# Cross-attention with four head groups per round: row and column tiles of the array, the division on GpSimd, the maxima of the context moved

## What is computed

```python
h, d = 16, 8                                   # heads, channels of a head
q = layernorm_per_head(x @ Wq.T + bq) * d ** -0.5
k = layernorm_per_head(y @ Wk.T + bk);  v = y @ Wv.T + bv     # y: context, 512 keys
attn = einsum('bihd,bjhd->bhij', q, k)
attn = where(mask, attn, -inf)
out = einsum('bhij,bjhd->bihd', softmax(attn), v) @ Wo.T + bo
```

## Time and profile before

| what | value |
|---|---|
| median of 3 runs | 739.34 us (737.47 to 740.51) |
| the profiled execution | 740.16 us |
| its span, first to last instruction | 738.3 us |
| busy: PE, DVE, ACT, POOL | 618.2, 498.4, 306.1, 144.8 us |
| mean granted clock of TensorE | 0.763 |

### The profile page before, as it was taken

The page is one execution under the profiler, slowest core; times in us unless marked ns, Lnnn a source line. Parts: engine busy times, 40 slices in busy tenths (PEclk is TensorE's granted clock), DMA queues, the critical chain, the costliest instruction groups (busy, mean ns, idle before and its releaser), DMA issues.

```text
span 738.3 us, 21781 instructions
## 1 busy us (share of the span) xinstructions
PE 618.2 (84%) x8501; PEld 476.5 (65%) x8501; DVE 498.4 (68%) x1962; ACT 306.1 (41%) x859; POOL 144.8 (20%) x177
## 2 busy tenths in 40 slices
PE   4969997876889758999899998997689888988866
PEld 3536665434678558888888888886466556655634
DVE  1697665477453467777777777774287888878883
ACT  2935453433365543333333333333445445544511
POOL 3330000420800000000000000000543564346500
PEclk9999999887799855555555555555599999999997
DMA  9700000000100200000000000000000000000000
GB/s 344 321 1 1 1 1 2 1 1 2 41 1 1 66 22 3 0 0 0 0 0 0 0 0 0 0 0 1 0 1 1 0 1 1 1 0 1 0 1 7
DMA packets 6057, 15.26 MB, mean 21 GB/s; under 512 B 2640, under 2 KB 3288, under 8 KB 5504
## 3 DMA queue, kind: packets, MB, share of 16 engines
q1 hardware_dynamic: 5296, 11.19, 4.1%
q10 hardware_dynamic: 720, 3.55, 1.2%
HBM read 14.60 MB, written 0.13 MB: 20 GB/s over the span
## 4 chain that ended last, share of the span: by engine, by line
PE 49%; DVE 30%; ACT 11%; issue 8%; DMA 1%; POOL 1%; DVEq 0%; SPq 0%; ACTq 0%
PE bank L1659 9%; PE bank L1732 7%; PE bank L1568 6%; PE bank L1386 4%; PE bank L1369 4%; ACT esp L661 3%; PE bank L1519 2%; DVE ssum L1122 2%; DVE T L1192 2%; ACT a L647 2%; ACT e L663 2%; PE bank L1377 2%; PE bank L1506 2%; DVE rz L1159 2%; DVE zs L1157 2%
## 5 line engine op out<-in xcount | busy, mean ns | idle before, releaser
L1568 PE MATMUL bank<-esp,qblk 128*128 128x1 f16 (+1 forms) x2048 | 66.6, 166 | 0.7 <-ACT esp L661 0.7
L1568 PE MATMUL bank<-hsp,kT 128*128 128x2 f16 x2048 | 63.6, 166 | 2.5 <-DVE hsp L1150 1.7
L1568 PEld LDWEIGHTS bank<-hsp,kT 128*128 128x128 f16 x2048 | 60.0, 104 | 3.5 <-DVE hsp L1147 1.7
L1568 PEld LDWEIGHTS bank<-esp,qblk 128*128 128x128 f16 x2048 | 61.3, 104 | 1.3 <-ACT esp L661 1.1
L647 ACT ACTIVATE a<-opre 128x4 f32<-128x4 f32 x64 | 13.1, 205 | 115.8 <-DVE opre L1110 115.8
L455 POOL MEMSET ctxT<- 128x128 f32 x1 | 0.3, 312 | 306.2 <-DVE xres L1166 306.2
L1192 DVE SCALAR_TENSOR_TENSOR T<-bank,bct,T 128x256 f32<-128x256 f32 x112 | 46.4, 475 | 1.3 <-PE bank L1745 1.3
L1179 DVE TENSOR_TENSOR_SCAN qblk<-ctxT,bank 128x512 f32<-128x512 f32 x32 | 37.6, 1208 | 13.5 <-PE bank L1732 13.1
L1568 PE MATMUL bank<-asp,lsp 128*128 128x4 f16 x768 | 30.7, 168 | 16.4 <-DVE asp L1112 16.4
L1568 PEld LDWEIGHTS bank<-asp,lsp 128*128 128x128 f16 x768 | 25.4, 105 | 27.9 <-DVE asp L1112 27.7
L1179 DVE TENSOR_TENSOR_SCAN w<-kT,bank 128x512 f32<-128x512 f32 x32 | 37.5, 1207 | 8.2 <-PE bank L1732 8.2
(11 more groups left out here) (327 smaller groups left out, 1471.1 us busy)
## 6 DMA issues: line engine op xcount, KB each, us to landing
w<-in_w_dram SPq DMA_DIRECT2D x2, 2048.0 KB
ctxT<-in_ctxT_dram SPq DMA_DIRECT2D x8, 256.0 KB, 12.9
wqkv<-in_qkvT_dram ACTq DMA_DIRECT2D x1, 1536.0 KB, 11.7
w<-in_mw_dram SPq DMA_DIRECT2D x1, 1024.0 KB, 5.1
lw<-in_lw_dram SPq DMA_DIRECT2D x1, 960.0 KB, 19.8
rows<-in_rows_dram ACTq DMA_DIRECT2D x1, 772.0 KB, 7.9
wqkv<-in_fw_dram SPq DMA_DIRECT2D x1, 532.0 KB, 3.3
T<-in_mask_dram ACTq DMA_DIRECT2D x1, 512.0 KB, 5.8
```

The source lines that it names most:

```text
L1568: return pe.matmul(out, lhsT, rhs, start=start, stop=stop, skip_group_check=True)
```

## The change

All 16 heads of a sequence are now handled in one round of four items, which fill the array by tiles.

- Queries: `qblk` keeps one 128 x 128 block per sequence. Rows 32g to 32g+31 hold group g. Four multiplications fill it (with the negated scale) instead of sixteen, and GpSimd's zeroing (line 381) is gone.
- Scores: four matmuls of 32 rows each, on rows 32g to 32g+31 of the array, into banks 0 to 3, issued one behind the other. They wait for all four maxima of the sequence before, since there is one set of banks.
- Scores are negated, so that the mask operation's minimum is the negated maximum, and line 841 is gone; ACT's exponential has scale -1 and works in place.
- The multiplication by the reciprocal moves from DVE to GpSimd, in place; DVE keeps the reciprocal. Items have six buffers (XR).
- Of the four copies of transposed blocks ACT makes three and DVE the fourth, behind the round's maxima. Eight buffers.
- Values: one `x_pv` per sequence, two rounds late, whose 16 matmuls go over the four column tiles in turn.
- `wmean` is computed on DVE between the first and the second round; GpSimd's lines 405 and 411 come behind its 32 multiplications.
- The eight maxima of the context move into self-attention's loop, one per block m behind `a_rope`; those of the LSTM's weights and the gathering follow that loop, and `partition_all_reduce` comes behind GpSimd's eight additions.
- In the last layer two semaphores (`r_gate`, `r_h`) are merged into `f_gate` and `f_h`; nothing else changes there.

```diff
@@ gpsimd
-            pool.memset(qblk[:, :, :, :, :], 0.0).then_inc(sem["mask_ready"], 1)
...
+            for i in range(B * XG):
+                pool.wait_ge(sem["x_rz"], i + 1)
+                pool.tensor_scalar(x_soft(i), x_soft(i), xrz[:, i:i + 1], 0.0, ALU.mult, ALU.add).then_inc(sem["x_norm"], 1)
             pool.wait_ge(sem["a_wmean"], 1)
@@ scalar
-                if i >= 2:
-                    act.wait_ge(sem["x_norm"], i - 1)
-                act.activation(T[:, 2 + i % 2, :], T[:, i % 2, :], ACT.Exp, bias=xneg[:, i:i + 1],
+                act.activation(x_soft(i), x_soft(i), ACT.Exp, scale=-1.0, bias=xneg[:, i:i + 1],
                                accum_out=xz[:, i:i + 1]).then_inc(sem["x_exp"], 1)
...
-            for i in range(B * XG + 2):
+                if i >= 2 * XG:
+                    act.wait_ge(sem["x_pv"], i // XG - 1)
+                act.activation(x_probT(i), bank[4 + i % 2][:, :], ACT.Copy).then_inc(sem["x_pt"], 1)
+
+            for i in range((B + 1) * XG):
                 if i < B * XG:
                     x_exp(i)
-                if i >= 2:
-                    x_copy_pt(i - 2)
+                if i >= XG and i % XG != XG - 1:
+                    x_copy_pt(i - XG)
@@ vector
+                dve.tensor_scalar(qblk[:, 0, :, h, :], T[:, 10, 0:TOK].rearrange("p (b s) -> p b s", b=B),
+                                  cst[:, C_HM + h:C_HM + h + 1], -XD ** -0.5, ALU.mult, ALU.mult) \
...
+                if i >= XR:
+                    dve.wait_ge(sem["x_tr"], i - XR + 1)
+                dve.tensor_tensor_reduce(x_soft(i), bank[g][:, :], maskb[:, b * SK:(b + 1) * SK],
+                                         1.0, -FLOOR, ALU.add, ALU.min, xneg[:, i:i + 1]).then_inc(sem["x_max"], 1)
...
+                dve.reciprocal(xrz[:, i:i + 1], xz[:, i:i + 1]).then_inc(sem["x_rz"], 1)
...
+            for b in range(B + 2):
+                for g in range(XG):
+                    i = b * XG + g
+                    if i < B * XG:
+                        x_max(i)
+                    if 1 <= i <= B * XG:
+                        x_norm(i - 1)
+                if b == 0:
+                    dve.wait_ge(sem["d_attn"], 32)
+                    step(dve.tensor_reduce(wmean[:, :], wqkv[:, 0:2 * AH * AD].rearrange("p (h d) -> p h d", d=AD), AX, ALU.add))
+                    dve.tensor_scalar(wmean[:, :], wmean[:, :], 1.0 / AD, None, ALU.mult).then_inc(sem["a_wmean"], 1)
+                if 1 <= b <= B:
+                    x_copy_pt(b * XG - 1)
+                if b >= 2:
+                    x_heads(b - 2)
@@ vector, self-attention's loop
+                if m < B:
+                    l_size(lmax[:, m:m + 1], ctxT[:, m * SK:(m + 1) * SK])
@@ tensor
+                for g in range(XG):
+                    own = slice(32 * g, 32 * g + 32)
+                    pe.matmul(bank[g][:, :], qblk[own, 0, b, :, :], kT[own, b * SK:(b + 1) * SK],
+                              start=True, stop=True).then_inc(sem["x_score"], 1)
...
                 for c in range(KC):
+                    for g in range(XG):
+                        ins = pe.matmul(bank[6 + b % 2][32 * g:32 * g + 32, 0:P], vx[:, b * KC + c, 32 * g:32 * g + 32],
+                                        x_probT(b * XG + g)[:, c * P:(c + 1) * P], start=(c == 0), stop=(c == KC - 1))
...
+            for b in range(B + 2):
+                if b < B:
+                    x_scores(b)
+                if b >= 2:
+                    x_pv(b - 2)
+                if 1 <= b <= B:
+                    for g in range(XG):
+                        x_transpose((b - 1) * XG + g)
```

More of the change, by code:

```diff
@@ L331, in transposed, with x_soft, x_probT, x_turned @@
             return n + 1 if n < LN_LAST else LN_LAST + 1
+        def x_soft(i):
+            return T[:, i % XR, :]
+        def x_probT(i):
+            return T[:, XR + i % (2 * XG), :]
+        def x_turned(eng, i):
+            if i % XG == XG - 1:
+                eng.wait_ge(sem["x_ptd"], i // XG + 1)
+            else:
+                eng.wait_ge(sem["x_pt"], i // XG * (XG - 1) + i % XG + 1)
         def nth(stream, t):
@@ L427, in _ @@
                                    ALU.mult, ALU.add).then_inc(sem["a_z"], 1)
+            pool.wait_ge(sem["l_stat"], 1)
+            pool.partition_all_reduce(lall[:, :], ltop[:, :], P, REDUCE.max).then_inc(sem["l_max"], 1)
             pool.wait_ge(sem["x_res"], 2)
@@ L823, in _ @@
                 k_hat(s)
-                if s >= 1:
-                    q_blocks(2 * (s - 1))
-            dve.wait_ge(sem["d_attn"], 32)
-            step(dve.tensor_reduce(wmean[:, :], wqkv[:, 0:2 * AH * AD].rearrange("p (h d) -> p h d", d=AD), AX, ALU.add))
-            dve.tensor_scalar(wmean[:, :], wmean[:, :], 1.0 / AD, None, ALU.mult).then_inc(sem["a_wmean"], 1)
+                if 1 <= s <= 4:
+                    q_block(s - 1)
             def x_max(i):
-                b = i // XG
+                b, g = divmod(i, XG)
@@ L866, in l_size @@
                 step.mark(dve.tensor_reduce(to, of, AX, ALU.max, apply_absolute_value=True))
-            for i in range(B * XG + 4):
-                if i < B * XG:
-                    x_max(i)
-                if 1 <= i <= B * XG:
-                    x_norm(i - 1)
-                if i >= 4 and (i - 4) % XG == XG - 1:
-                    x_heads((i - 4) // XG)
-                if i < B:
-                    l_size(lmax[:, i:i + 1], ctxT[:, i * SK:(i + 1) * SK])
-                if i == 12:
-                    dve.wait_ge(sem["l_w"], 4)
-                    for k, (at, end) in enumerate(((14, 15), (13, 14), (4, 13))):
-                        l_size(lmax[:, B + k:B + k + 1], lw[:, at * D:end * D])
-            step.sync()
-            step(dve.tensor_reduce(ltop[:, 0:1], lmax[:, 0:B], AX, ALU.max))
-            dve.tensor_copy(ltop[:, 1:4], lmax[:, B:B + 3]).then_inc(sem["l_stat"], 1)
+            for b in range(B + 2):
[13 more added lines that the diff above has]
+                    x_heads(b - 2)
             dve.wait_ge(sem["x_oT"], B)
@@ L929, in _ @@
                     a_rope(m - 1)
+                if m < B:
+                    l_size(lmax[:, m:m + 1], ctxT[:, m * SK:(m + 1) * SK])
+            dve.wait_ge(sem["l_w"], 4)
+            for k, (at, end) in enumerate(((14, 15), (13, 14), (4, 13))):
+                l_size(lmax[:, B + k:B + k + 1], lw[:, at * D:end * D])
+            step.sync()
+            step(dve.tensor_reduce(ltop[:, 0:1], lmax[:, 0:B], AX, ALU.max))
+            dve.tensor_copy(ltop[:, 1:4], lmax[:, B:B + 3]).then_inc(sem["l_stat"], 1)
             dve.wait_ge(sem["a_rope"], 8)
```

90 lines of the change are left out of this document (32 added, 58 removed).

## The result

| what | before | after |
|---|---|---|
| median of all runs beside each other | 738.40 us (737.39 to 740.51, 4 runs) | 708.01 us (705.90 to 710.02, 4 runs) |
| ratio of the times, 95% interval | | 0.9585 [0.9548, 0.9621] |
| the profiled execution, its span | 740.16, 738.3 us | 708.04, 706.2 us |
| busy: PE, DVE, ACT, POOL | 618.2, 498.4, 306.1, 144.8 us | 574.1, 478.9, 299.5, 161.7 us |
| mean granted clock of TensorE | 0.763 | 0.748 |

What follows compares the result with a forecast made beforehand. PE alone was taken to bound cross-attention; after the change, a DVE-ACT loop of waits. Stage -30.2, bias +0.4 and maxima +2.3 sum to -27.5 us on 740.16, giving 712.7, forecast 713; range 706 to 727.

Steps and rivals of the forecast that it cites:

- the stage: Cross-attention, up to the last `x_heads`: predicted to end at 95.0 instead of 125.2 us, so -30.2 us.
- Scores and values: PE's tiled matmuls per sequence: scores 1.08 us instead of 4.24, values 0.97 instead of 3.96.
- The round: One sequence of four items in cross-attention: a loop of waits between DVE and ACT, 5.65 us.
- rival 3: Cross-attention rounds: shorter waits, a round takes ACT's 4.6 us, five rounds save 5, total 708; chance 0.08.
- They wait for nobody: Next sequence's scores on PE: start at the fourth maximum, long before needed, take 1.1 us, and wait for nobody.
- The third round at half clock: Cross-attention's third round: PE at half clock is the bound, 7.7 us with gaps, fourth maximum at 59.2.
- Rival 1: Cross-attention: clock stays at half, all rounds from the second on at 7.73 us, total 726; chance 0.18.
- Drain: End of cross-attention, from the last maximum through the last sequences' copies and heads: 7.6 us, to 95.0.
- The bias beside GpSimd: DVE's bias operation (line 886) behind cross-attention, slowed beside GpSimd's subtraction: +0.4 us, bounds 0 and 1.1.
- `partition_all_reduce` isn't needed until the third layer: 0: GpSimd's reduction over partitions, moved behind its eight additions: claimed to cost 0 us.
- The maxima in the loop: Context maxima on DVE in self-attention's loop: one of two fits idle time, +2.3 us over eight, bounds 0 and 5.6.
- The division on GpSimd at nothing: Cross-attention's division moved to GpSimd: 3.6 to 4.2 us per round beside 5.65, cost nothing unless above 1.4 each.

Runs made afterwards that it cites:

- memset late: Changed kernel with GpSimd's zeroing of qblk for self-attention moved behind its eight additions; 702.38 us, ratio 0.9513.
- division on VectorE: Changed kernel with the 32 divisions moved back from GpSimd to VectorE, in place behind each reciprocal; 715.6 us.
- heads later: Changed kernel with VectorE's two reductions that collect a sequence's heads moved behind the next round's first maximum and its reciprocal; 709.03 us, ratio 0.9584.
- maxima moved in the kernel before: Kernel before with only the maxima of context and weights, and GpSimd's reduction over partitions, moved in and behind self-attention's loop; 740.49 us, ratio 1.0015.
- two items later: Changed kernel with reciprocal and division two items behind the maximum instead of one; 707.62 us, ratio 0.9566.
- three banks: Changed kernel with three PSUM banks in turn for the transposes instead of two, and one for the values instead of two; 712.23 us, ratio 0.9629.
- both: Changed kernel with three PSUM banks for transposes, one for values, and reciprocal and division two items behind the maximum; 698.88 us, ratio 0.9465.

## Why the prediction was right, and where its steps were off

Forecast 713, measured 708.0, in the range. The sum said -27.5 us; the profiled executions differ by -32.1. The 4.6 us between them are misses of both signs: the stage gave 3.7 more, self-attention's loop cost 1.5 less, the rest gave 1.4, and the layer norm cost 2.0 more.

- **Scores and values: right.** 1.14 and 1.08 us for 1.08 and 0.97. The row nearest in form, which overlaps five times, pointed the right way; against 3.60 on the whole array the scores overlap 3.2 times. The pair of tiles would have given 1.97 for the values.
- **The round: 5.27, not 5.65.** The loop over VectorE and ScalarE was named rightly, but its terms were durations laid end to end. Their starts lie closer: the copy starts 0.72 us behind the exponential, the next exponential 0.49 behind the copy of 0.59, and the operation behind VectorE's copy of 0.69 starts 0.61 after it. Five rounds make 1.9 us. That is the small form of rival 3, whose bound of 4.6 wasn't reached.
- **"They wait for nobody": wrong.** Scores do wait, in TensorE's list behind transposes that wait for a bank, and VectorE's copy waits for these transposes too. It cost nothing in the sum, because that loop is as long as the other, which was luck. It is why two ways to shorten VectorE's side of the round gave nothing.
- **The third round at half clock: wrong.** 7.8 us were set for it, from fourth maximum to fourth maximum; it took 5.3 (ends 51.9 and 57.2). The scores from 45.72 and the transposes behind them kept TensorE busy without a gap, and from 49.28 the clock was 1.00. Rival 1 fell with it, and the steady rounds kept 1.00. The Trainium skill, "TensorE: Matmul & The Clock Gate", Part 4 (PE-mode transpose), says that transposes don't count as work for the clock gate. The trace disagrees plainly for holding the clock; for raising it the stretch speaks against the rule without settling it, since 2 us of scores stand at its start.
- **Drain: right**, 7.8 for 7.6 us. The stage: -33.9 for -30.2, which is 2.5 (third round) and 1.9 (rounds), less 0.7 for the start and the drain.
- **The bias beside GpSimd: wrong place.** It took 0.35 us, undisturbed, as GpSimd was just through. The collision came 3 us later, in the layer norm, with GpSimd's memset, and cost 2.4 us instead of 0.4. The step that failed is "`partition_all_reduce` isn't needed until the third layer: 0". It isn't, but before, GpSimd came to its next operation only 7.21 us behind it, and so the memset missed the norm, as rows of the kernel before show (the norm's pair took 0.61 us); the queue behind a moved step wasn't followed.

```profile
125.57 0.39 POOL L415 PARTITION_ALL_REDUCE lall<-ltop  x1 [77.86 <-DVE ltop L883]
...
128.38 0.61 DVE L783 TENSOR_SCALAR xn<-xres,mv,rs 128x128 f32<-128x128 f32 x2 [0.60 <-ACT rs L491]
...
133.16 0.71 POOL L418 TENSOR_TENSOR xbias<-xres,rows 128x256 f32<-128x256 f32 x1 [7.21 <-issue]
133.83 3.50 POOL L420 MEMSET qblk<- 128x4096 f32 x1
```

- **The maxima in the loop: +0.8 for +2.3.** A block went from 3.12 to 3.25 us, by 0.13 and not by 0.31. VectorE now has next to no idle time in a block: 0.60 us for the maximum and 2.65 for the rest, so before there were 2 x (3.12 - 2.65) = 0.94 us idle in two blocks. The prediction let only one of two maxima use that; both did. The rows from one `a_z0` to the next, 117.92 to 121.17:

```profile
117.92 0.74 DVE L914 SCALAR_TENSOR_TENSOR T<-bank,vec,T 128x512 f32<-128x512 f32 x1
118.58 0.68 DVE L924 TENSOR_TENSOR T<-T,cst 128x512 f32<-128x512 f32 x1
119.18 0.68 DVE L926 TENSOR_TENSOR T<-bank,cst 128x512 f32<-128x512 f32 x1
119.97 0.69 DVE L930 TENSOR_TENSOR kT<-T 128x512 f32<-128x512 f32 x1
120.58 0.68 DVE L875 TENSOR_REDUCE lmax<-ctxT 128x1 f32<-128x512 f32 x1
121.17 0.74 DVE L914 SCALAR_TENSOR_TENSOR T<-bank,vec,T 128x512 f32<-128x512 f32 x1
```

- **The division on GpSimd at nothing: right**, 0.69 us each; on VectorE it would have cost 7.6 us.
- **The rest** of the difference, -32.1 against -30.7 at the loop's end, wasn't in the sum. Half lies ahead of the first scan and half behind it, and what made it is open; more full clock ahead of the scan it isn't (64.9 us, before 68.3).

## What to carry to other kernels

When an engine's share falls away, lay out every loop of waits that is left, through the in-order lists too: two of nearly one length hide each other, so each fix alone reads as no gain, and only both together show. Add starts, not durations, for chains on one engine. And a removed or moved instruction lets everything behind it in its list run earlier: ask what that will stand beside.

## What the runs showed of the hardware

**A memset on GpSimd holds up some of VectorE's operations.** VectorE's pair of float32 operations with one tensor from SBUF to SBUF took 3.00 us beside the memset and ended 0.15 us behind it (94.39 + 3.00, 93.73 + 3.51), and 0.60 without. Beside GpSimd's subtraction a division on VectorE took 3.27 us instead of 0.49. But where the memset stood late, VectorE's multiplications of two tensors and its maxima took 0.68 us beside it (128.03), as without it. The Trainium skill, "SBUF — State Buffer", "SBUF: two separate sides", describes this as an exclusive lock on a port pair that both engines share, held for a whole instruction; the runs agree for the operations that were held up, and show it for one on GpSimd that only writes.

**Full clock behind transposes.** TensorE is busy without a gap from 45.72, first with 2 us of scores; 47.72 to 49.28 is transposes alone but for the tail of the scores, and full clock follows. Whether the scores alone would have done it no run shows.

**Unchanged code moves by 3.5 us with the clock's stretches.** From the end of self-attention's loop to the first scan, all kernels run the same instructions, but for the maxima of the LSTM's weights with their gathering and GpSimd's reduction and memset, which stand there in some and ahead of it in others. Four profiles (memset late, division on VectorE, heads later, maxima moved in the kernel before) have 78.5 us of full clock there and took 364.7 to 365.3 us; four (the changed kernel, two items later, three banks, both) have 64.9 us and took 368.0 to 368.5. Those between, with 68.3 to 75.1, don't follow an order (366.4 to 368.7). The changed kernel and the one with the memset late part mostly within 33 us behind the loop's end: the first is at half clock from 158.50 to 172.16, the second from 158.64 to 165.47 only, and is 2.9 us ahead there. Another place is just ahead of the scan, first in the changed kernel, then with the memset late (11.9 us each, up to the scan):

```profile
489.10:501.00 11.90, 5.61 (x18) 4.00 (x18) 2.88 (x7) 5.29 (x13) 7.28 (x8) 0.50 0.00 0
```

```profile
482.90:494.80 11.90, 5.10 (x22) 3.28 (x22) 2.88 (x7) 6.26 (x15) 7.26 (x8) 0.64 0.00 0
```

Executions of one kernel differ in the same way: the kernel before took 742.29 us at a mean clock of 0.757 and 736.38 at 0.775, the one with both loops open 704.26 at 0.741 and 698.88 at 0.755.

A local gain of 2 or 3 us can thus come out as 1 or 6 in the time, as it did for the maxima moved (2.6, measured 1.1) and for the memset (2.4, measured 5.6). What sets these stretches off wasn't tested. In such a kernel a small edit is better judged by its own place in the trace, and by the time between executions of nearly one granted clock.
